# Attention in a mixed convolution/attention block: PSUM banks shared out anew between score tiles, score rows and turned maxima

## The reference

```python
# h = layernorm_c(x); 4 images of 1024 tokens, 12 heads of 16 channels
attn = einsum('bqd,bkd->bqk', q, k) / sqrt(16)
attn = attn + rel_bias_h[:, :, :, :, None] + rel_bias_w[:, :, :, None, :]
out  = softmax(attn, axis=-1) @ v
x    = x + out @ Wp + bp
x    = x + quantised_ffn(layernorm(x))      # 192 -> 768 -> 192, 4-bit steps
```

## Time and profile before

| what | us |
|---|---|
| median of 3 runs (906.38 to 907.9) | 906.96 |
| the profiled execution's own time | 904.3 |
| its span, first to last instruction | 902.5 |
| PE busy (88% of the span) | 791.0 |
| DVE busy (82%) | 743.8 |
| ACT busy (62%) | 558.8 |
| POOL busy (47%) | 423.4 |
| mean granted clock of PE, share of full speed | 0.949 |

### The profile page before, as it was taken

One profiled execution on the slowest core, in us unless ns is written; L12 is line 12 of the kernel. 1 busy time (PEld: TensorE's weight loads), 2 busy tenths in 40 slices (PEclk: granted clock), 3 DMA queues, 4 the chain that ended last, 5 costly groups with the idle time before them and its releaser, 6 DMA issues. The chain is left out here.

```text
span 902.5 us, 15297 instructions
## 1 busy us (share of the span) xinstructions
PE 791.0 (88%) x5848; PEld 407.7 (45%) x5848; DVE 743.8 (82%) x1493; ACT 558.8 (62%) x609; POOL 423.4 (47%) x263
## 2 busy tenths in 40 slices
PE   5899554479999999999999999999999999678874
PEld 2555454134444444444444444444444442256653
DVE  6998855498989988988998999998888894069995
ACT  1333345027777777777777777777777778447773
POOL 3777794436364454637263735445373324112220
PEclk9999788589999999999999999999999999889986
DMA  7676599999439392948567493939395000433411
GB/s 193 212 226 206 164 300 374 256 194 208 90 88 188 77 200 60 205 85 190 111 147 154 109 191 74 198 68 201 63 206 96 13 12 12 134 105 123 140 36 53
DMA packets 65675, 130.06 MB, mean 144 GB/s; under 512 B 9465, under 2 KB 45306, under 8 KB 57146
## 3 DMA queue, kind: packets, MB, share of 16 engines
q1 hardware_dynamic: 57634, 115.95, 56.2%
q10 hardware_dynamic: 7968, 13.13, 4.2%
HBM read 89.73 MB, written 34.60 MB: 138 GB/s over the span
## 5 line engine op out<-in xcount | busy, mean ns | idle before, releaser
L1065 DVE TENSOR_REDUCE at_piece_neg<-at_r_ps 128x1 f32<-128x512 f32 x768 | 482.8, 682 | 68.1 <-PE at_r_ps L935 64.7
L1028 ACT ACTIVATE at_probs<-at_s_ps 128x1024 f32<-128x1024 f32 x384 | 371.9, 1021 | 130.6 <-PE at_s_ps L956 129.3
L935 PE MATMUL at_r_ps<-op_mix_k,op_mix_q 128*128 128x256 f16 (+1 forms) x1920 | 282.0, 257 | 29.9 <-DMA op_mix_q<-bias_parts 17.8
L935 PEld LDWEIGHTS at_r_ps<-op_mix_k,op_mix_q 128*128 128x128 f16 x1920 | 148.2, 98 | 295.1 <-DVE at_piece_neg L1065 194.1
L850 POOL COPY op_mix_q<-op_mix_q 2x4096 f16<-2x4096 f16 x48 | 172.6, 3596 | 231.0 <-ACT op_mix_q L1033 230.5
L956 PE MATMUL at_s_ps<-op_mix_q,op_mix_k 128*128 128x512 f16 x768 | 227.7, 380 | 1.1 <-ACT at_probs L1028 0.5
L970 PE MATMUL at_o_ps<-at_probs,op_v_u 128*32 128x512 f32 x1536 | 204.2, 604 | 0.0
L218 POOL MEMSET op_mix_q<- 2x10240 f32 x12 | 103.5, 8627 | 0.6
L1033 ACT ACTIVATE op_mix_q<-at_r_ps 2x1024 f16<-2x1024 f16 x48 | 48.5, 1011 | 60.7 <-PE at_r_ps L946 60.7
L956 PEld LDWEIGHTS at_s_ps<-op_mix_q,op_mix_k 128*128 128x128 f16 x768 | 73.4, 98 | 19.6 <-ACT at_probs L1028 10.7
L854 POOL TENSOR_TENSOR at_o_sb<-at_o_sb,at_inv_rows 128x512 f32<-128x512 f32 x24 | 30.7, 1280 | 86.2 <-DVE at_inv_rows L1092 86.2
(11 more groups left out here) (121 smaller groups left out, 674.4 us busy)
## 6 DMA issues: line engine op xcount, KB each, us to landing
op_mix_q<-qk_parts SPq DMA_DIRECT2D x48, 640.0 KB, 10.7
op_mix_q<-bias_parts SPq DMA_DIRECT2D x120, 120.0 KB, 10.3
op_mix_q<-bias_parts SPq DMA_DIRECT2D x72, 128.0 KB, 10.3
bias_parts<-op_mix_q ACTq DMA_DIRECT2D x8, 1024.0 KB, 13.1
qk_parts<-op_mix_q SPq DMA_DIRECT2D x24, 256.0 KB, 2.3
v_rows<-pr_v_st SPq DMA_DIRECT2D x8, 768.0 KB, 4.1
op_mix_k<-qk_parts SPq DMA_DIRECT2D x48, 128.0 KB, 13.1
op_v_u<-v_rows SPq DMA_DIRECT2D x12, 512.0 KB, 14.2
```

What stands on the lines that cost most here:

```text
L935: last = pe.matmul(r_bank("piece", at)[:, first % GROUP:first % GROUP + n], mix_q[owner.buf][:, variant, j, qt * P:(qt + 1) * P], mix_k[ow ...
L1028: act.activation(probs[n % PRING][:, 2 * pair:2 * pair + 2, :], s_ps[pair][:, :, :], ACT.Exp).then_inc(exp_done, 1)
L1065: dve.tensor_reduce(piece_neg[half][:, i:i + 1], r_bank("piece", at)[:, :], AX_X, ALU.max, negate=True).then_inc(reduced, 1)
```

## The change

- `s_ps` becomes a ring of three single banks (SRING), one head's scores each. Every `scores` matmul waits for its bank and signals for itself, and `exps` has four operations of 512 columns a step in place of two of 1024.
- The turned maxima leave the ring of the pieces and take a turn in the ring of the scores. One pair of semaphores, s_filled and s_taken, counts both; `use_of` holds the order of uses.
- `r_ps` becomes two pairs of banks (RRING). A score row of 1024 keys stands in one pair and is reduced by one DVE operation. 32 rows a unit take the place of 64 pieces; `join_max` has two operations in place of three.
- Within a step PE's order is: score 0, row, score 1, score 2, row, score 3, weigh. No row stands behind `weigh` any more.

```diff
-    PIECES = QUAD * KT * 2
-    PER_STEP = PIECES // STEPS
+    ROWS = QUAD * 2 * TILES
+    PER_STEP = ROWS // STEPS
     LEAD = 3
-    RING = 3
+    SRING, RRING = 3, 2
...
-        s_ps = [ph.ps(f"s_ps{i}", [P, 2, GROUP], F32) for i in range(2)]
-        r_ps = [ph.ps(f"r_ps{i}", [P, GROUP], F32) for i in range(RING)]
+        s_ps = [ph.ps(f"s_ps{i}", [P, GROUP], F32) for i in range(SRING)]
+        r_ps = [ph.ps(f"r_ps{i}", [P, 2, GROUP], F32) for i in range(RRING)]
...
+        ROWS_BEFORE = (0, 1, 1, 2, 2)
...
+        use_of = {("turn", 0, 0): 0, ("turn", 0, 1): 1}
+        for u in range(UNITS):
             for n in range(STEPS):
                 for half, pair in turned_at(n):
...
+                    if half == 1 or u + 1 < UNITS:
+                        use_of["turn", u * 2 + 1 if half else (u + 1) * 2, pair] = len(use_of)
+                for j in range(QUAD):
+                    use_of["scores", u * STEPS + n, j] = len(use_of)
...
+            def score_row(unit, at):
+
+                owner, i = (unit, at) if at < ROWS else (unit.after(1), at - ROWS)
+                j, qt = i // TILES % QUAD, i // (ROWS // 2) * TILES + i % TILES
+                count = unit.u * ROWS + at
+                need(pe, reduced, count - RRING + 1)
                 for variant, first, n in ops.SEGMENTS:
-                    if first // GROUP == kh:
-                        last = pe.matmul(r_bank("piece", at)[:, first % GROUP:first % GROUP + n],
-                                         mix_q[owner.buf][:, variant, j, qt * P:(qt + 1) * P],
-                                         mix_k[owner.buf][:, j, first:first + n], start=True, stop=True)
-                last.then_inc(piece_done, 1)
+                    last = pe.matmul(r_ps[count % RRING][:, first // GROUP, first % GROUP:first % GROUP + n],
+                                     mix_q[owner.buf][:, variant, j, qt * P:(qt + 1) * P],
+                                     mix_k[owner.buf][:, j, first:first + n], start=True, stop=True)
+                last.then_inc(row_scored, 1)
 
             def turn(unit, half, pair):
 
                 owner = unit if half == 1 else unit.after(1)
+                use = turn_use(owner, half, pair)
                 pe.wait_ge(neg_done, (owner.u * 2 + half) * 2 + pair + 1)
-                wait_bank(pe, unit, "maxima", half * 2 + pair)
+                need(pe, s_taken, use - SRING + 1)
                 for t in range(2 * TILES):
-                    last = pe.transpose(max_rows(half * 2 + pair)[:, t * P:(t + 1) * P], neg_max[half][:, pair * 2 * TILES + t, :], ident16[:, :])
-                last.then_inc(max_rowed, 1)
+                    last = pe.transpose(max_rows(use)[:, t * P:(t + 1) * P], neg_max[half][:, pair * 2 * TILES + t, :], ident16[:, :])
+                last.then_inc(s_filled, 1)
 
             def scores(unit, n, j):
                 half, kt = n // KT, TILE_ORDER[n % KT]
-                pair = j // 2
-                step = unit.u * STEPS + n
-                if j % 2 == 0:
-                    need(pe, exp_done, step * 2 + pair - 1)
+                use = use_of["scores", unit.u * STEPS + n, j]
+                need(pe, s_taken, use - SRING + 1)
                 keys, queries = slice(kt * P, (kt + 1) * P), slice(half * GROUP, (half + 1) * GROUP)
-                last = pe.matmul(s_ps[pair][:, j % 2, :], mix_k[unit.buf][:, j, keys], mix_q[unit.buf][:, ops.VARIANT_OF[kt], j, queries],
-                                 start=True, stop=True)
-                if j % 2 == 1:
-                    last.then_inc(scores_done, 1)
+                pe.matmul(s_ps[use % SRING][:, :], mix_k[unit.buf][:, j, keys], mix_q[unit.buf][:, ops.VARIANT_OF[kt], j, queries],
+                          start=True, stop=True).then_inc(s_filled, 1)
 
...
                     for j in range(QUAD):
-                        for at in todo[BEFORE[j]:BEFORE[j + 1]]:
-                            piece(unit, at)
                         if n % KT == 0 and j % 2 == 0:
-                            pe.wait_ge(max_in, rows_in(unit.u, n // KT * 2 + j // 2))
+                            pe.wait_ge(s_taken, turn_use(unit, n // KT, j // 2) + 1)
                         scores(unit, n, j)
-                    for at in todo[BEFORE[QUAD]:AFTER]:
-                        piece(unit, at)
+                        for at in todo[ROWS_BEFORE[j]:ROWS_BEFORE[j + 1]]:
+                            score_row(unit, at)
...
-                    for at in todo[AFTER:]:
-                        piece(unit, at)
...
-                for pair in range(2):
-                    act.wait_ge(scores_done, step * 2 + pair + 1)
-                    act.activation(probs[n % PRING][:, 2 * pair:2 * pair + 2, :], s_ps[pair][:, :, :], ACT.Exp).then_inc(exp_done, 1)
+                for j in range(QUAD):
+                    use = use_of["scores", step, j]
+                    act.wait_ge(s_filled, use + 1)
+                    act.activation(probs[n % PRING][:, j, :], s_ps[use % SRING][:, :], ACT.Exp).then_inc(s_taken, 1)
...
-            def reduce_piece(unit, at):
-                half, i = at // (PIECES // 2) % 2, at % (PIECES // 2)
-                need(dve, piece_done, unit.u * PIECES + at + 1)
-                dve.tensor_reduce(piece_neg[half][:, i:i + 1], r_bank("piece", at)[:, :], AX_X, ALU.max, negate=True).then_inc(reduced, 1)
+            def reduce_row(unit, at):
+                half, i = at // (ROWS // 2) % 2, at % (ROWS // 2)
+                count = unit.u * ROWS + at
+                need(dve, row_scored, count + 1)
+                dve.tensor_reduce(row_neg[half][:, i:i + 1], r_ps[count % RRING][:, :, :].rearrange("p h t -> p (h t)"),
+                                  AX_X, ALU.max, negate=True).then_inc(reduced, 1)
 
             def join_max(unit, half, pair):
 
                 owner = unit if half == 1 else unit.after(1)
                 rows, count = slice(pair * 2 * TILES, (pair + 1) * 2 * TILES), (owner.u * 2 + half) * 2 + pair + 1
-                dve.wait_ge(reduced, owner.u * PIECES + half * (PIECES // 2) + (pair + 1) * (PIECES // 4))
-                need(dve, max_rowed, rows_in(owner.u - 1, half * 2 + pair))
-                halves = piece_neg[half][:, pair * (PIECES // 4):(pair + 1) * (PIECES // 4)].rearrange("p (r k) -> p r k", k=2)
-                dve.tensor_tensor(row_neg[half][:, rows], halves[:, :, 0], halves[:, :, 1], ALU.min)
-                dve.tensor_tensor(neg_max[half][:, rows, 0], halves[:, :, 0], halves[:, :, 1], ALU.min).then_inc(neg_hi, 1)
+                dve.wait_ge(reduced, owner.u * ROWS + half * (ROWS // 2) + (pair + 1) * (ROWS // 4))
+                if owner.u:
+                    dve.wait_ge(s_filled, turn_use(owner.after(-1), half, pair) + 1)
+                dve.tensor_tensor(neg_max[half][:, rows, 0], row_neg[half][:, rows], row_neg[half][:, rows], ALU.min).then_inc(neg_hi, 1)
```

More of the change, by code:

```diff
@@ L734, in phase_attention @@
         consts, loaded, N_LOADS = ops.consts, ops.loaded, ops.N_LOADS
-        piece_neg = [ph.sb(f"piece_neg{h}", [P, PIECES // 2], F32) for h in range(2)]
         row_neg = [ph.sb(f"row_neg{h}", [P, QUAD * TILES], F32) for h in range(2)]
@@ L775, in each_unit, with rows_of @@
                 emit(Unit(u, u // NQUAD, u))
-        def pieces(n):
-            at = PIECES // 2 + (LEAD + n) * PER_STEP
+        def rows_of(n):
+            at = ROWS // 2 + (LEAD + n) * PER_STEP
             return list(range(at, at + PER_STEP))
@@ L802, in joined_at, with turn_use, max_rows @@
             return [key for key, step in JOIN_AT.items() if step == n]
[L804 to L810, removed]
+        use_of = {("turn", 0, 0): 0, ("turn", 0, 1): 1}
+        for u in range(UNITS):
             for n in range(STEPS):
                 for half, pair in turned_at(n):
[L814 to L842, removed]
+                    if half == 1 or u + 1 < UNITS:
+                        use_of["turn", u * 2 + 1 if half else (u + 1) * 2, pair] = len(use_of)
+                for j in range(QUAD):
+                    use_of["scores", u * STEPS + n, j] = len(use_of)
+        def turn_use(unit, half, pair):
+            return use_of["turn", unit.u * 2 + half, pair]
+        def max_rows(use):
+            return s_ps[use % SRING][:, :].bitcast(F16)[0:2, :]
         @block.gpsimd
@@ L848, in spread_max @@
                 rows = mix_q[unit.buf][MAX_ROW:MAX_ROW + 2, :, heads, cols]
-                pool.wait_ge(max_in, rows_in(unit.u, half * 2 + pair))
+                pool.wait_ge(s_taken, turn_use(unit, half, pair) + 1)
                 pool.tensor_copy(rows[:, 1:, :, :], rows[:, 0:1, :, :].to_broadcast([2, ops.VARIANTS - 1, 2, GROUP])).then_inc(max_spread, 1)
@@ L965, in weigh @@
                 step = unit.u * STEPS + n
-                pe.wait_ge(exp_done, step * 2 + 2)
+                pe.wait_ge(s_taken, use_of["scores", step, QUAD - 1] + 1)
                 if at == 0:
@@ L981, in _ @@
                         turn(BEFORE_FIRST, 0, pair)
```

(40 more changed lines are left out.)

12 lines of the change are left out of this document (2 added, 10 removed).

## The result

The changed kernel takes 904.5 us (median of 20 runs, 903.26 to 906.29) where the kernel before, timed beside it, takes 906.44: a ratio of 0.9983, interval 0.9976 to 0.9991. It is faster, by 1.9 us between the medians and 1.5 by the ratio. The forecast was a loss of 2.3.

A forecast was written before the change was run, and what follows sets the result against it. PE was taken to set the pace. Units 0 to 10 (-0.3 us), the stretch before unit 0 (-1.4) and the last unit (+4.0) summed to +2.3 on the 906.96 median: 909.2 us, range 904.5 to 915.

The forecast's parts named there:

- Part 1: Units 0 to 10: all three PE stalls for DVE's reduces go, -1.07 us a unit (bounds 0 to -1.07).
- Part 2: Turn right behind weigh: one array-shape change in three saved at four turns, -0.38 us a unit (bounds 0 to -0.38).
- Part 3: Turn steps: third score waits for ACT's copy of the maxima, +1.28 and +0.14 us a unit (bounds +1.1 to +2.0).
- Part 4: Before unit 0: cheaper row reduces -1.8 us, longer first wait +0.4, sum -1.4 (bounds -2.5 and +0.4).
- Part 5: Last unit, from step 5 without rows: three banks make steps 2.44 us, not 2.22; +4.0 in all (bounds +3 and +7).
- the new wait bites less: Rival, turn steps: ACT releases the maxima before PE needs the bank; 894 us, or 902 for half; chance 0.12.
- never became the bound: Rival, steps of four exponentials: at 0.67 us each ACT becomes the bound, 917 us; chance 0.12.
- The clock in the last unit: Rival, last unit: PE busy only 78%, so its clock falls; 914 to 925 us; chance 0.08.

The follow-up runs named there:

- the two edits: Changed kernel with second row one place earlier (902.28 us), or weigh ahead of the last score in turn steps (902.02 us); both, in turn steps, 886.65 us.

## Why the prediction was wrong

- **Part 1 (DVE's stalls, -1.07 a unit)** came in whole. The reason given held three causes: fewer reduces, a shorter join and a longer lead. The run with halved reduces shows that the first two are not needed; the lead was not separated from the maxima's leaving that ring and from PE's new order.
- **Part 2 (the turn's place, -0.38 a unit) is the step that failed, by its size.** It held that `weigh` "pays for its own change whatever follows". It does not: a score or piece starts 1.00 behind the start of `weigh`, the turn 0.883. So a turn saves 0.21 (0.095 and 0.116), not 0.095: -0.84 a unit. In 11 units that is 5 us beyond the forecast. Its bound of -0.38 was too narrow: no row of before had a turn behind `weigh`, and a larger gain was excluded without a reason.
- **Part 3 (the new wait, +1.42 a unit)** was right in place and mechanism. Two turn steps wait 0.30 as forecast (0.32). The other two wait 0.53, not 0.39: `take_out` starts when `weigh` has ended, and with the turn now 0.116 nearer to `weigh`, the copy behind `take_out` starts 0.87 and not 0.71 after the turn, which is most of the difference. So part of what part 2 gave beyond the forecast was taken back: 2 x 0.30 + 2 x 0.53 = +1.66. The taking back is no accident: the nearer turn causes it. The other half of the reasoning, that score 3 just clears the first exponential (2.37 against 2.28 behind the turn), came true, and the run with the second row one place earlier shows how near that was to a second wait: it met it.
- Sum of a unit: -1.07 - 0.84 + 1.66 = -0.25, measured -0.294, forecast -0.03. Eleven units gave -2.8 (unit 0 had one stall fewer to lose) and not -0.3. This is most of the miss of 3.7 us in the traces. By the medians the miss is 4.7 (909.2 against 904.5), of which 0.5 is the starting point: the forecast began from a median of three runs, 906.96, where 20 runs gave 906.44.
- **Part 4 (before unit 0)** gave -2.4, not -1.4. The cheaper reduces give 1.35 to 1.80 of it against 1.8 forecast: the run with halves took 34.78, and three executions with the changed kernel's instructions up to this point took 33.33, 33.43 and (seven banks at the end) 32.98. The rest, about 0.97 (35.75 to 34.78) in spite of the longer first wait of 0.43, came with the banks and PE's order. DVE's idle time behind a turn is one place where it shows, first before, then after:

```profile
183.20 1.29 DVE L1065 TENSOR_REDUCE at_piece_neg<-at_r_ps 128x1 f32<-128x512 f32 x2 [0.54 <-PE at_r_ps L935]
```

```profile
183.02 6.88 DVE L1030 TENSOR_REDUCE at_row_neg<-at_r_ps 128x1 f32<-128x1024 f32 x6 [0.26 <-PE at_r_ps L904]
...
190.22 9.14 DVE L1030 TENSOR_REDUCE at_row_neg<-at_r_ps 128x1 f32<-128x1024 f32 x8
```

  Behind the second turn (0.35 before) it has gone altogether, and in the run with halves DVE is idle behind neither. The 0.26 varies between executions of the same instructions: it is 0.36 in the changed kernel's repetition, at a granted clock of 0.50 from 180 to 185, and nothing with seven banks at the end, at 0.91; here the clock was 0.73, and in the kernel before 0.50. So the clock may have a share in this stretch, which no run separates from that of the banks. The forecast had left this idle time out.
- **Part 5 (the last unit, +4.0)** measured +3.8, with steps of 2.46 for 2.44, a turn step of 3.54 for 3.7 and one behind `take_out` of 2.59 for 2.7. The run with seven banks shows that the ring's depth is the cause.
- **The rivals.** That the new wait bites less did not happen: it bit more. ACT's exponentials follow each other in 0.48 to 0.60 and never became the bound. (The price of that rival was added up wrongly: 0.4 twice a unit is 8.8 us in eleven units, not 4.4, which makes 921 and not 917.) The clock in the last unit stayed at 1.00 with PE busy 87% of a window (17.32 of 20 us), although it paused at a bank in every plain step. The forecast's 78% was also not "between" its two rows, 95% (18.99 of 20) and 86% (4.31 of 5), but below both. What the Trainium skill tells of another kernel and was cited for that rival ("TensorE: Matmul & The Clock Gate", the section on psum-queue depth-cycling), a clock that swings under such pauses, did not happen here. The time of 904.5 lies on the range's lower edge; the range was too narrow below, since part 2 had its lower bound set at its own estimate.

## What to carry to other kernels

When a small transfer through another engine shares a ring with the main work, walk the ring from its issue: with N banks, N - 1 other uses stand before the bank is wanted again, and their work must last as long as the round trip (at a turn here 1.42 us of work against 1.71). Where two waits stand one behind the other, taking away one only moves it: the two edits gave 0.14 and 0.00 us a unit singly and 1.48 together. The value of a place in an instruction order lies in both neighbours; where the pair has never stood side by side in a trace, leave both signs open. A ring that was deep enough while other work filled the steps can be too shallow where that work ends; banks that fall idle there are the cheap cure.

## What the runs showed of the hardware that was not expected

- `weigh` (eight fp32 passes in 32 columns each) hands over to the fp16 turn (2 columns of weights) 0.88 after its own start, in 45 cases of the changed kernel and 44 of the kernel with the turn moved. To a score of 128 columns it hands over only after 1.00 (144 cases in the changed kernel), and to a piece likewise (179 in the kernel before). On the way in, from a score to `weigh` (0.309) and from a piece to the turn (0.203), each pays about 0.095 over the interval inside a run of equal matmuls.
- A reduce over two PSUM banks costs no more than its length: 1.217 for 1024 elements where 0.682 for 512 and 0.167 for 8 put 1.20, and 1.13 to 1.14 from one to the next in a queue.
- The kernel with halved reduces, the changed kernel and its repetition gave the same unit of 48.85 us to a hundredth, with DVE busy 43.96 of it in the first and 41.89 in the second: where PE's own work and ACT's durations set the pace, 2.07 us of DVE's work a unit leave no trace in the time.
